# Cosine product of the rotation on VectorE for all 16 token tiles instead of the last eight

## What is computed

```python
def _rope(x, cos, sin):
    x1, x2 = jnp.split(x, 2, axis=-1)
    rot = jnp.concatenate([-x2, x1], axis=-1)
    return x * cos[None, :, None, :] + rot * sin[None, :, None, :]
...
qkv = jnp.einsum('bsh,oh->bso', hidden_states, w_qkv) + b_qkv
...
q = _rope(q, cos, sin)
k = _rope(k, cos, sin)
```

## Time and profile before

| | |
|---|---|
| median of 3 runs | 1745.68 us (1744.61 to 1749.37) |
| the profiled execution's own time | 1748.59 us |
| its span in the trace | 1746.4 us (2.2 us lie around it) |
| TensorE busy | 1601.1 us, 92% of the span |
| VectorE, ScalarE, GpSimd busy | 916.0, 649.0, 239.1 us |
| mean granted TensorE clock | 0.97 of full speed |

### The profile page before, as it was taken

The page is one execution under the profiler, slowest core; times in us unless marked ns, Lnnn a source line. Parts: engine busy times, 40 slices in busy tenths (PEclk is TensorE's granted clock), DMA queues, the critical chain, the costliest instruction groups (busy, mean ns, idle before and its releaser), DMA issues.

```text
span 1746.4 us, 27217 instructions
## 1 busy us (share of the span) xinstructions
PE 1601.1 (92%) x9280; PEld 739.6 (42%) x9280; DVE 916.0 (52%) x1622; ACT 649.0 (37%) x919; POOL 239.1 (14%) x349
## 2 busy tenths in 40 slices
PE   1788999999999879999899899999999999999998
PEld 0233444444445534444444444433444444444443
DVE  7887413324137777777677677773243241232212
ACT  4662112211121125676666576667221211212111
POOL 0310000000005542232222232212000000000000
PEclk9899999999999958999999999999999999999999
DMA  9404400000000000000000000000600000000000
GB/s 388 145 0 182 188 0 1 1 0 1 0 0 1 1 31 2 2 2 2 3 2 2 3 2 2 3 2 2 253 1 0 0 25 0 0 24 0 25 0 24
DMA packets 14804, 57.59 MB, mean 33 GB/s; under 512 B 2992, under 2 KB 2992, under 8 KB 14192
## 3 DMA queue, kind: packets, MB, share of 16 engines
q1 hardware_dynamic: 14704, 56.23, 8.3%
HBM read 40.63 MB, written 15.20 MB: 32 GB/s over the span
## 4 chain that ended last, share of the span: by engine, by line
PE 78%; DVE 13%; issue 4%; ACT 3%; DMA 1%; POOL 1%; SPq 0%; DVEq 0%; ACTq 0%; POOLq 0%
PE ps L1239 30%; PE ps L1260 14%; PE ps L1429 7%; PE ps L1473 7%; PE ps L1455 6%; DVE rowmax L1135 4%; PE ps L1544 3%; PE ps L1342 3%; PE ps L1286 2%; PE ps L1374 2%; PE ps L1432 2%; DMA w_raw<-w1t 1%; ACT qa L726 1%; PE ps L1233 1%; PE ps L1480 1%
## 5 line engine op out<-in xcount | busy, mean ns | idle before, releaser
L1135 DVE TENSOR_REDUCE rowmax<-ps 128x1 f32<-128x512 f32 (+3 forms) x608 | 381.4, 658 | 133.5 <-PE ps L1429 74.9
L768 ACT ACTIVATE probs<-ps 128x1024 f32<-128x1024 f32 (+3 forms) x384 | 292.5, 812 | 171.7 <-PE ps L1455 171.5
L1239 PE MATMUL ps<-xt_hi,w_all 128*128 128x512 f16 x896 | 282.4, 388 | 42.8 <-DVE w_all L925 19.8
L1429 PE MATMUL ps<-ka,qa 96*128 96x512 bf16 (+3 forms) x768 | 243.9, 348 | 38.7 <-DVE rowmax L1135 34.3
L1455 PE MATMUL ps<-qa,ka 99*128 99x512 bf16 (+3 forms) x768 | 190.2, 331 | 9.2 <-issue 7.2
L1013 DVE SCALAR_TENSOR_TENSOR hb<-ps,scal,silub 128x512 f32<-128x512 f32 x56 | 42.0, 750 | 266.6 <-PE ps L1239 266.6
L1239 PE MATMUL ps<-xt_lo,w_all 128*128 128x512 f16 x448 | 174.1, 389 | 0.0
L1473 PE MATMUL ps<-probs,vs 128*32 128x512 f32 (+3 forms) x1536 | 164.1, 499 | 2.4 <-ACT probs L768 1.5
L1429 PEld LDWEIGHTS ps<-ka,qa 96*128 96x128 bf16 x768 | 75.2, 99 | 190.9 <-DVE rowmax L1135 154.6
L1239 PEld LDWEIGHTS ps<-xt_hi,w_all 128*128 (+1 forms) x896 | 89.4, 100 | 156.5 <-issue 45.8
L1239 PE MATMUL ps<-xt_hi,w13b_all 128*128 128x512 f16 x448 | 138.0, 379 | 0.8 <-DVE x L1213 0.8
(11 more groups left out here) (140 smaller groups left out, 1999.7 us busy)
## 6 DMA issues: line engine op xcount, KB each, us to landing
spill<-w_all SPq DMA_DIRECT2D x1, 10752.0 KB, 28.7
w13b_all<-spill SPq DMA_DIRECT2D x1, 7168.0 KB, 19.8
x<-x_in SPq DMA_DIRECT2D x4, 1024.0 KB, 5.3
y_out<-x SPq DMA_DIRECT2D x4, 1024.0 KB, 4.3
wbase<-m1t SPq DMA_DIRECT2D x4, 896.0 KB, 12.5
w_raw<-w1t SPq DMA_DIRECT2D x4, 896.0 KB, 14.1
wbase<-m3t SPq DMA_DIRECT2D x4, 896.0 KB, 23.8
w_raw<-w3t SPq DMA_DIRECT2D x4, 896.0 KB, 24.1
```

Source lines behind the costliest of these rows:

```text
L768: nc.scalar.activation(probs[u % PBUF][:, 2 * pair:2 * pair + 2, 0:q1 - q0], ps[:, 2 * pair:2 * pair + 2, 0:q1 - q0], ACT.Exp, scale=SM_SC ...
L1135: nc.vector.tensor_reduce(dst, ps[:, PASS1 + r % 2, 0:w * len(heads)].rearrange("p (h w) -> p h w", w=w), AX.X, ALU.max).then_inc(p1_read, 1)
L1239: last = mm(ps[:, bank, :], w[a][:, k, bass.ts(t, P)], xt[b][:, k, :], start=(k == 0 and n == 0), stop=(k == HB - 1 and n == 2))
L1429: last = mm(ps[:, PASS1 + r % 2, n * w:(n + 1) * w], qa[v][0:ROWS, h, qt * P:(qt + 1) * P], ka[v][0:ROWS, k0:k0 + w], start=True, stop=not ...
```

## The change

The cosine product of tiles 0 to 7 goes from GpSimd to VectorE, so that all 16 tiles have it there. The count that `rotated(i)` gives, of GpSimd's instructions before the sum of tile `i` may start, becomes two for each tile. The rest is as it was: operands, buffers and sizes are the same.

```diff
 def rotated(i):
-    return 3 * (i + 1) - max(0, i + 1 - SEQ_TILES)
+    return 2 * (i + 1)
...
-            if i < SEQ_TILES:
-                nc.gpsimd.tensor_tensor(out=c4, in0=r, in1=table(cos, 0, HEAD), op=ALU.mult).then_inc(rot_ready, 1)
             for lo in (0, H2):
                 nc.gpsimd.tensor_tensor(out=s4[:, :, :, lo:lo + H2], in0=r[:, :, :, H2 - lo:HEAD - lo],
                                         in1=table(sin, lo, lo + H2), op=ALU.mult).then_inc(rot_ready, 1)
...
             add_bias(i)
             if i:
                 rotate(i - 1)
-            if i >= SEQ_TILES:
-
-                dve.wait_ge(raw_ready, 2 * (i + 1))
+            dve.wait_ge(raw_ready, 2 * (i + 1))
+            if i:
                 dve.wait_ge(qk_ready, i)
-                raw = qkv_raw[i % 2][:, :, 0:QK].rearrange("p g (h d) -> p g h d", d=HEAD)
-                factor = cos[:, i % SEQ_TILES, :].unsqueeze(1).unsqueeze(1)
-                chain(nc.vector.tensor_tensor(out=rot_c[:, :, :].rearrange("p g (h d) -> p g h d", d=HEAD), in0=raw,
-                                              in1=factor.to_broadcast([P, SEQ_PAIRS, QK // HEAD, HEAD]), op=ALU.mult))
+            raw = qkv_raw[i % 2][:, :, 0:QK].rearrange("p g (h d) -> p g h d", d=HEAD)
+            factor = cos[:, i % SEQ_TILES, :].unsqueeze(1).unsqueeze(1)
+            chain(nc.vector.tensor_tensor(out=rot_c[:, :, :].rearrange("p g (h d) -> p g h d", d=HEAD), in0=raw,
+                                          in1=factor.to_broadcast([P, SEQ_PAIRS, QK // HEAD, HEAD]), op=ALU.mult))
```

## The result

| | before | changed |
|---|---|---|
| median of 14 runs each | 1747.19 us (1744.5 to 1749.37) | 1751.89 us (1747.38 to 1754.0) |
| the profiled execution: own time, span | 1748.59, 1746.4 us | 1751.14, 1749.4 us |

The ratio is 1.0023, with a 95% interval of 1.0015 to 1.0032. That is 4.0 us (2.6 to 5.6) more. The change costs a little, and the interval leaves no doubt about the sign. About half of that (1.5 us) is the starting point: three executions gave 1745.68 us for the kernel before, fourteen gave 1747.19.

What follows compares the result with a forecast made beforehand. VectorE's late layer norm, for which TensorE waits, was taken to bound the projection stage. Terms 0.57 + 0.86 + 0.79 + 1.05 = 3.27 us on a median of 1745.68 gave 1749.0 us, range 1745.0 to 1753.5.

Steps and rivals of the forecast that it cites:

- The mechanism: Projection stage, first eight tiles: VectorE is late with the layer norm, TensorE waits 8.7 us for `xnorm`, rising to about 12.
- Tile 0: Product between `add_bias(0)` and `xnorm`: the `xnorm` end at 535.58 us, the transposes could start at about 535.55; no cost.
- Tile 8's row: Unchanged tile with the new form, used as price list: second `xnorm` ends 2.82 us behind the product's start.
- Tile 1: Product between `rotate(0)` and the two `xt_lo` delays the second transposes ahead of tile 3, and `add_bias(3)`: +0.57 us.
- Tile 3: Product behind `rotate` costs +1.05 us, `rotate(2)` no longer waiting for GpSimd's late sine product gives -0.19: together +0.86.
- Tile 4: From `rotate(3)` to the end of the second `xnorm`: 2.95 us before, 3.74 in tile 8's form, so +0.79.
- the rule in full: A less busy GpSimd hands `xnorm` all its time back: tile 4 -0.17 us instead of +0.79, sum 2.3.
- Tiles 5 and 6: Product delays `xt_lo` by 0.86 us, covered because TensorE reaches the transposes 2.2 us later; some 0.6 if uncovered.
- Tile 7: From `rotate(6)` to `norm_stats`, 0.73 us becomes 1.78: +1.05.
- The low clock: Rival behind both pauses ahead of tiles 6 and 10: TensorE stays at low clock longer, +6.0 us, 1754.9 in all; 13%.
- The rival in which GpSimd had set the pace: Product takes 1.70 us on GpSimd, 0.83 on VectorE; eight times the difference is 7.0 us, so 1738.7, faster; 6%.
- The hidden case: Rival: idle time later in the stage, or a low-clock stretch ending 3 us sooner, absorbs VectorE's delay; 1745.7 us; 10%.

Runs made afterwards that it cites:

- the halves by tile: Two kernels timed against the one before: product on VectorE except in tiles 3, 4, 7, ratio 1.0001; on VectorE in 3, 4, 7, 8 to 15, 1.0016.

## Why the prediction was right

- **The mechanism** (VectorE late with `xnorm`, TensorE idle ahead of tiles 6 and 10) was right, and the halves by tile put the cost where the sum had it. The longest pause is 5.04 us where about 5.4 was forecast. But TensorE's wait in total went to 10.1 us and not to about 12. The matmuls behind the pauses start 1.62 and 3.12 us later (2.2 and 3.3 were forecast for the transposes). The idle time grew by less, because all eight transposes now stand behind a pause (2.12 us), where four of them had stood inside it.
- **Tile 0:** nothing, right. The four `xnorm` even took 2.87 us instead of 4.22. Tile 8's row (3.17 for the four) was a little too dear for tile 0, because there GpSimd's split of operands runs beside it. So `add_bias(1)` came 0.37 us earlier.
- **Tile 1:** +0.31 instead of +0.57, for the same reason: `xt_lo` started 0.47 us later than before, not 0.86. The idle time that was forecast ahead of tile 3's transposes does not show as such; the eight of them took 1.23 us instead of 1.04.
- **Tile 3:** +0.84 up to `norm_stats` as forecast (0.86), less 0.32 behind it. The term was mis-sized, since it looked at the product alone. GpSimd's product of before had also held up the first small instruction of the statistics.
- **Tile 4:** +0.79, to the hundredth. The choice between the rule in full and tile 8's row was right: of `xnorm`'s 1.76 us beside GpSimd's cosine product, 1.08 stayed beside the sine products. By the hand-back in full this term would have been -0.17.
- **Tiles 5 and 6:** covered, right, and where the cover went (with the product back on GpSimd in 3, 4 and 7) the wait of 1.65 us appeared.
- **Tile 7:** +0.71 instead of +1.05, the same 0.33 as in tile 3.
- **The low clock** was put at the same 0.92 us as before for each pause. It cost 0.80 more behind the first and 0.05 more behind the second. That rival was right in kind, and its share is a quarter of the measured stage difference, but far from its +6.0.

The path terms come to 0.31 + 0.52 + 0.79 + 0.71 = 2.33 us, not 3.27. The clock added 0.85. The difference in the profile, 3.16, came out close to the forecast because these two errors offset each other, and that is luck. The timed difference of 4.0 us (2.6 to 5.6) holds both 3.16 and 3.27. The rival in which GpSimd had set the pace is refuted by the result, which is not faster, and by the kernel with the product on GpSimd in six tiles, which was no slower. GpSimd does lie on the path in places: 0.19 us at `rotate(2)` of the kernel before, and about half a microsecond with the pauses filled. The hidden case is refuted by the interval.

## What to carry to other kernels

Price a moved instruction by its place: between the last point where its engine waited for the bound one and the next that the bound one waits for, it costs in full, and elsewhere nothing as long as the bound engine comes late enough to cover it. An unchanged tile of the same kernel that already has the new form is the best price list, but look at what else runs beside it. Compare two profiles mark by mark and not by their ends, so that a change of clock far from the edit is not booked to the edit. Before statistics or other long blocks are moved off one wait, list every other result of that engine that now stands behind them.

## What the runs showed of the hardware

- VectorE's `TENSOR_SCALAR` was held until GpSimd's running product ended, whatever its size: 128x4 took 0.50 us instead of 0.17 and ended 0.02 us behind that product, 128x512 took 1.76 instead of 0.54 and ended 0.29 behind it. With `TENSOR_TENSOR` the one that started second paid. VectorE's cosine product of tile 8 started at 578.34 and took its usual 0.83 us, GpSimd's sine product started at 578.37 and took 1.50 instead of 0.86. At the end of the stage it is the other way round, and VectorE's sum takes 1.69 us instead of 0.81 (before):

```profile
619.48 1.15 POOL L485 TENSOR_TENSOR parts_q<-left,parts_q 128x512 bf16<-128x512 f32 x1
619.62 1.69 DVE L1101 TENSOR_TENSOR store<-rot_c,rot_s 128x640 f32<-128x640 f32 x1 [1.62 <-POOL rot_s L525]
```

  The Trainium skill's GPSIMD Engine Reference (opening table, SBUF interfaces) names both kinds of contention, that with a 2-port mode of VectorE and that with two SBUF inputs. These rows agree for two inputs; that `TENSOR_SCALAR` ran in such a mode is not shown by them.
- The low clock behind a pause of TensorE is no fixed price. The 24 matmuls that take 3.9 us at the full clock took 4.83 behind 4.1 us of idle time, 5.62 behind 5.04, 4.90 behind another 5.04, 5.83 behind 4.33, 5.88 behind 3.88, and 3.9 behind 2.87. Twelve matmuls near the end of the stage took 3.64 us in one kernel and 1.96 in another. A single profile can be off by more than 1 us from this alone.
- With TensorE's pause behind the stage filled, the clock still fell within 5 us of it and stayed at 0.50 up to 670 us, with TensorE busy for 3.2 to 4.8 of every 5 us at that clock.
